# An attention and expert kernel: the key-value step one batch later, one pending projection at the end of the batch, and one scatter then two

## The reference, cut to what matters

```python
x  = L0_attn_x                                   # 16 batches x 256 rows x 128, f32
xn = layernorm(x)
out = x + attention(xn) + experts(xn)

# attention: 16 heads of 8 columns, 64 random features per head
q, k, v = xn@Wq + bq, xn@Wk + bk, xn@Wv + bv     # split into heads
qp = relu(q @ rw) + 1e-6                         # per head 8 -> 64
kp = relu(k @ rw) + 1e-6
kv  = einsum('bhsf,bhsd->bhfd', kp, v)
qkv = einsum('bhsf,bhfd->bhsd', qp, kv)
norm = einsum('bhsf,bhf->bhs', qp, kp.sum(axis=2))
attention = (qkv / (norm[..., None] + 1e-6)).reshape(B, S, D) @ Wo + bo

# experts: 8 experts, hidden size 512, each row goes to its best one
logits = xn @ wr + br
gate = p1 / (p1 + p2)                            # the two largest probabilities
experts = gate * (gelu(xn @ w1[e] + b1[e]) @ w2[e] + b2[e])   # e = argmax(logits)
```

## Time and profile before

| | us |
|---|---|
| median of 3 runs | 218.1 (217.13 to 218.14) |
| the profiled execution | 218.47 |
| its span, first to last instruction | 216.4 |
| PE busy | 201.2 (93%) |
| POOL busy | 140.7 (65%) |
| DVE busy | 131.1 (61%) |
| ACT busy | 124.1 (57%) |
| mean granted clock of PE | 0.982 of full |

### The profile page before, as it was taken

How to read it: one execution, slowest core, us unless ns; L and a number is a source line. 1 busy time by engine, 2 the same in 40 slices (tenths; PEclk the granted TensorE clock), 3 DMA queues, 4 the chain that set the end, 5 groups by cost and what they waited for, 6 DMA issues and landing times. The chain is left out here.

```text
span 216.4 us, 6736 instructions
## 1 busy us (share of the span) xinstructions
PE 201.2 (93%) x2291; PEld 162.8 (75%) x2291; DVE 131.1 (61%) x422; ACT 124.1 (57%) x293; POOL 140.7 (65%) x163
## 2 busy tenths in 40 slices
PE   6789996989999999999999999999999999999960
PEld 6466764556676676767766767999999999999960
DVE  5877744779777666677777673554544445544440
ACT  3366988345546655556556585656665555666520
POOL 2498941232188877878778510078888888888885
PEclk9999999699999999999999999999999999999996
DMA  4929999990012111112114882199999999999141
GB/s 134 272 48 266 213 116 255 299 233 6 3 49 64 64 61 55 46 52 64 64 50 114 270 231 70 48 232 199 178 207 215 204 215 199 194 213 198 10 36 10
DMA packets 32192, 29.53 MB, mean 136 GB/s; under 512 B 5505, under 2 KB 24481, under 8 KB 32161
## 3 DMA queue, kind: packets, MB, share of 16 engines
q1 hardware_dynamic: 25520, 24.88, 46.1%
q0 software_dynamic: 6640, 4.24, 12.3%
HBM read 20.17 MB, written 11.49 MB: 146 GB/s over the span
## 5 line engine op out<-in xcount | busy, mean ns | idle before, releaser
L412 POOL DMA_INDIRECT out<-k_all,slots_all x39 | 61.1, 1567 | 23.6 <-issue 23.3
L738 ACT ACTIVATE q_all<-feat,w_slot 128x128 f32<-128x128 f32 x156 | 44.5, 368 | 28.3 <-PE feat L591 20.8
L591 PE MATMUL feat<-v_all,w_slot 128*128 128x128 f32 x312 | 41.2, 275 | 0.0
L380 POOL DMA_INDIRECT sorted_x<-rows_all,place_i x32 | 31.9, 995 | 13.0 <-PE feat L477 8.0
L591 PEld LDWEIGHTS feat<-v_all,w_slot 128*128 128x128 f32 x312 | 38.0, 192 | 0.0
L695 ACT ACTIVATE k_feat<-feat 128x1024 f32<-128x1024 f32 x16 | 16.4, 1024 | 19.8 <-PE feat L477 19.8
L702 ACT ACTIVATE q_feat<-feat 128x1024 f32<-128x1024 f32 x16 | 16.4, 1027 | 15.5 <-PE feat L488 15.5
L884 DVE TENSOR_SCALAR q_feat<-feat 128x1024 f32<-128x1024 f32 x16 | 19.6, 1225 | 8.8 <-PE feat L488 8.8
L488 PE MATMUL feat<-q_all,rw_bd 32*128 32x256 f32 x256 | 18.8, 408 | 3.8 <-DVE k_feat L877 1.9
L337 POOL TENSOR_SCALAR rows_all<-x_all,meanvar,rstd 128x128 f32<-128x128 f32 x21 | 16.8, 811 | 7.8 <-DVE rstd L770 7.7
L601 PE MATMUL o_bank<-w_sb,q_all 128*128 x160 | 21.2, 275 | 0.0
(11 more groups left out here) (120 smaller groups left out, 314.5 us busy)
## 6 DMA issues: line engine op xcount, KB each, us to landing
w_slot<-w1x SPq DMA_DIRECT2D x39, 258.0 KB
sorted_x<-ones_f SPq DMA_DIRECT2D x1, 2535.0 KB, 20.2
x_all<-in_x SPq DMA_DIRECT2D x8, 256.0 KB, 4.1
w1x<-in_w SPq DMA_DIRECT2D x1, 2048.0 KB, 25.6
out<-res SPq DMA_DIRECT2D x16, 128.0 KB
slots_all<-sorted_x SPq DMA_DIRECT2D x23, 65.0 KB
out<-k_all,slots_all POOLq DMA_INDIRECT x39
slots_all<-sorted_x SPq DMA_DIRECT2D x1, 520.0 KB, 5.1
```

The costliest lines, as they stand in the source:

```text
L380: pool.indirect_dma_start(sorted_x, bass.IndirectOffsetOnAxis(ap=place_i[:, t:t + 1], axis=0), rows_all[:, t, :], None).then_inc(x_moved, 16)
L412: pool.indirect_dma_start(out_rows, bass.IndirectOffsetOnAxis(ap=slot_rows[j % SLOT_RING][:, D + 1:XW].bitcast(I32), axis=0), y_sb[j % Y_R ...
L591: ins = pe.matmul(bank[:, a * P:(a + 1) * P], w1_slot[j % W1_RING][:, a * P:(a + 1) * P], xsT[j % X_RING][:, :], start=True, stop=True)
L738: act.activation(hidden_T[j % H_RING][:, a * P:(a + 1) * P], hid_bank[j % HID][:, a * P:(a + 1) * P], ACT.Gelu, bias=w1_slot[j % W1_RING][ ...
```

## The change

In stage 2 KV of a batch is issued one pass later: `key_values(i-1)` between O and QF; the last one follows the loop. WO moves from before QF to the end of the pass. On DVE `mask_kv(i-1)` stands ahead of `q_relu(i)`, `residual` is taken one pass later (`i-5`), and three pieces of the routing go from before `q_relu` to after `token_rows`. On POOL the scatters of a pass are one at KF and two at QF instead of two and one (the total is 32 as before), `out_bias(i-1)` comes after those two, and the sixteen `add_out_bias` are done in the passes 0 to 3, four each. In stage 1 POOL normalises 2, 1 and 2 tiles of the chunks 1 to 3 instead of 3 each, and ACT saves the first transposed chunk before the second square root.

```diff
-KF_MOVES = {i: 2 for i in range(FIRST_MOVES, 15)}
-QF_MOVES = {i: 1 for i in range(FIRST_MOVES, 14)}
+KF_MOVES = {i: 1 for i in range(FIRST_MOVES, 14)} | {14: 2}
+QF_MOVES = {i: 2 for i in range(FIRST_MOVES, 14)}
...
-NORM = [0] + [3] * (CHUNKS - 1)
+NORM = [0, 2, 1, 2] + [3] * (CHUNKS - 4)
@@ POOL, the loop over the batches
                 pool.wait_ge(kf_ps, i + 1)
                 moves(KF_MOVES.get(i, 0))
-                if i >= 1:
-                    out_bias(i - 1)
                 if i + 1 < NBATCH:
                     spread_v(i + 1)
                 pool.wait_ge(qf_ps, i + 1)
                 moves(QF_MOVES.get(i, 0))
-                add_out_bias(i)
+                if i >= 1:
+                    out_bias(i - 1)
+                if i < FIRST_MOVES:
+                    for b in range(NBATCH // FIRST_MOVES * i, NBATCH // FIRST_MOVES * (i + 1)):
+                        add_out_bias(b)
@@ PE, the loop over the batches
                 if i >= 2:
                     outputs(i - 2)
+                if i >= 1:
+                    key_values(i - 1)
+                q_features(i)
+                if i >= 2:
+                    turn_outputs(i - 2)
+                if i >= 1:
+                    turn(i)
                 if i == 4:
                     pe.wait_ge(placed, 2)
                     pe.wait_ge(wo_in, 16)
                 if i >= 4:
                     out_project(i - 4)
-                q_features(i)
-                if i >= 2:
-                    turn_outputs(i - 2)
-                if i >= 1:
-                    turn(i)
-                key_values(i)
+            key_values(NBATCH - 1)
@@ ACT, stage 1
             deviation(0)
+            save_xnT(0)
             deviation(1)
-            save_xnT(0)
             deviation(2)
@@ DVE, the loop over the batches
-                if i == 1:
-                    count_slots()
-                if i == 2:
-                    place_rows()
-                if i == 3:
-                    place_gates()
-                if i >= 4:
-                    residual(i - 4)
+                if i >= 5:
+                    residual(i - 5)
+                if i >= 1:
+                    mask_kv(i - 1)
                 if i == 4:
                     compare_slots()
...
                 if i >= 2:
                     token_rows(i - 2)
-                mask_kv(i)
                 if i == 1:
+                    count_slots()
                     find_first()
+                if i == 2:
+                    place_rows()
+                if i == 3:
+                    place_gates()
+            mask_kv(NBATCH - 1)
+            residual(NBATCH - 5)
```

## The result

The changed kernel took 220.24 us (median; 219.97 to 220.54) where the kernel before took 218.10: a ratio of 1.0109, with a 95% interval of 1.0077 to 1.0141. The forecast was 216.8, faster. Two later comparisons, on two more chips, gave 1.0095 (1.0064 to 1.0126) and 1.0121 (1.0079 to 1.0164). It is about 1% slower each time.

What follows compares the result with a forecast made beforehand. PE's own work was taken to bound the attention loop, the relu chain close behind. Terms 0.9 + 0.2 - 1.35 - 2.2 + 0.2 + 0.7 + 0.2 = -1.35 gave 217.1 us profiled, 216.8 median; range 215.2 to 219.9.

Steps and rivals of the forecast that it cites:

- The loop, passes 5 to 14: Attention loop: about 5.57 us a pass instead of 5.87; -1.35 for passes 5 to 7, -2.2 for 8 to 14.
- KF(2): Start of the attention: lower clock until about 44.4 us puts KF(2) at 47.3 instead of 46.37, 0.9 later.
- KF(1): Start of the attention: KF(1) no longer waits behind KV(0), its input ready at about 40.4 us against 40.88.
- Passes 2 to 4: Early attention passes: 17.3 us instead of 17.07, +0.2, with place_rows making one pass 0.5 longer.
- The first slot: After the loop: +0.7 behind KF(15) as KV(15) follows the loop, +0.2 for the sorted rows' later load.
- Stage 1: Before the attention: fewer POOL tiles let the third chunk's transposes start sooner; 0.1 us gained, bounds 0.8 less to 0.3 more.
- KF completes late: Rival, attention loop: the pair of scatters holds KF's completion back by 0.65, a pass is 5.8, total 219.8 us; chance 0.26.
- The clock rises in time: Rival, start of attention: lower clock ends at 41.4 as before, KF(2) at 45.9, total 215.4 us; chance 0.16.
- The change does not do what it says: Rival: O and KV do not join (1.4 us back) and sorted rows land late (0.5), total 218.6 us; chance 0.11.

Runs made afterwards that it cites:

- the kernel with three edits: Changed kernel with KV(0) back in pass 0, one output-bias addition per pass and weight loads behind the store of batch 8: 221.05 us, 1.0113 of the kernel before.
- the dummies: Changed kernel with 17 dummy transposes behind KF(0) and 12 behind QF(0) in pass 0: 217.08 us, 0.9964 of the kernel before.

## Why the prediction was wrong, step by step

- **The loop, passes 5 to 14: right.** A pass was forecast at 5.57 and took 5.54. O and KV do join. KF to QF is 2.96 to 2.98, forecast 3.0. The rule of the Trainium skill that only a change of the tiling mode drains the engine (TensorEngine Tiling (Array Packing), Key Properties) agrees with this trace: O is followed by KV after 0.89, the same 16 matmuls that took 1.00 ahead of a group with other tiles. These terms gave 3.75 us where 3.35 was expected.
- **KF(2), +0.9 forecast, +2.26 measured: the mechanism right, one bound wrong.** QF(1) was put at 45.0 and started at 45.11. The next step failed: "I expect the lower clock until about 44.4", and so "KF(2) 2.6 behind it". The half clock lasted until 47.1, QF(1) took 2.09 instead of 1.15, and KF(2) came 3.52 behind it. I had read the length of the stretch from one fall and one rise; in other profiles it is 0, 3.4 or 6.8 us. The term should have had the whole of pass 1 at the lower clock as its bound. With it, KF(2) would have come out at 48.5 and the sum 1.2 higher. (The prediction also calls a rule of the Trainium skill a voice against this part; as it words the rule, the rule supports the cost that it computed.)
- **KF(1) gained nothing by losing KV(0).** The prediction gave the kernel before 40.88 for it, held by KV(0), and 40.4 without. It stood there because KV(0) itself ran at half clock; in the profiles at full clock KF(1) follows it at 40.40 to 40.45 with 0.73 to spare. The step removed a cover for PE and no cost.
- **Passes 2 to 4, +0.2 forecast, +1.32 measured: a cost left out.** "`place_gates` is shorter and costs nothing" and, of POOL, "free": each was costed by itself, and at the durations of the kernel before. `count_slots`, the third piece that moves, has no price in the prediction at all, and its pass has the largest miss: passes 2 to 4 were put at 5.6, 6.1 and 5.6 and took 6.25, 6.08 and 6.06. Only `place_rows`, the piece that was costed, came out as forecast. Before, the additions stood one by one; four in a row now cover just the stretch in which DVE's steps run between the relus. The pair costs 18.39 - 17.25 = 1.14, and vanishes with either part: 17.25 with the additions spread, 17.12 with the steps back at their old place.
- **The first slot, +0.9 forecast, +2.31 measured.** The issue of the rows was forecast at KF(14) + 9.7 = 126.7 and was at 126.19. What failed is "the rows need some 2.3 to land": 2.3 was the landing on idle DMA engines, and the order put it right behind six loads of weights. The slot at KF(15) + 6.52, without that, is the 6.55 of the prediction.
- **Stage 1** gave 0 of the expected 0.1: KF(0) at 34.55, before 34.49.
- **The rivals.** "KF completes late" did not happen in the first measurement, and did on two other chips, at first with the price that it was given: 0.5 to 0.55 late, 5.64 and 5.71 a pass, where the prediction's chain gives 5.66 to 5.71. At 0.65 it gives 5.8, and the kernel with three edits took 5.97, since KV was late as well, which the rival left out. Its total of 219.8 also holds a slip: three passes of 5.8 are 17.4 and not 17.8, so the rival's own time is 219.4. "The clock rises in time" is what the dummies made: KF(2) at 45.73, forecast 45.9. "The change does not do what it says" is out: the order does what it says, and the rows did land late, its second half; the slot lost 1.4 more than forecast where the rival gave 0.5.
- **The sum.** -1.35 forecast; +1.36 for the clock, +1.12 for passes 2 to 4, +1.41 for the slot, -0.4 for the loop and the rest: +2.1. All three misses are of one kind, a duration taken over from another place: the steps and the landing from where their neighbours were idle, the half clock from the one stretch in which it had been seen.

The range ended at 219.9, and 220.24 lies outside. The prediction had one or two bad terms at a time, and none of them was passes 2 to 4; three moderate ones together were not in it.

## What to carry to other kernels

A duration from a trace holds together with what ran beside it: when a step is moved, look up what the other engines, the DMA queues and the clock do at its new place. Moving work out of a place where an engine waits gains nothing there and may lower PE's clock; the work left in the hole is worth keeping. And when a reordering is a large gain in its loop and a loss at both ends, take the ends back one by one: here the new order with KV(0), the routing steps and the start of the weight loads put back was 0.7 and 0.9% faster than the kernel before on two chips without late groups, where the whole change was 1% slower. On a chip with late groups it was level, with dummies that themselves cost some time. A reordering is therefore worth measuring on more than one chip.

## What was not expected of the hardware

- Small DVE operations beside POOL's tensor operations took 0.43 to 0.66 us instead of 0.17, while POOL's 0.70 did not grow (four in 2.78).
- The stretch at half clock behind the same waits of PE lasted 3.4 or 6.8 us in profiles of kernels with the same code up to there, and nothing in between; with KV(0) in pass 0 also 0.
- A group of matmuls that completes while POOL issues scatters can reach the other engines 0.5 to 1.3 us late, and the matmuls behind it are stretched (QF 1.15 to 1.96 or 2.34). It came on some chips for an order that showed none on others: for the changed kernel in two comparisons of three, with the scatter at the same distance from KF (0.16 and 0.20 us behind its start in the two profiles with late groups, 0.16 in the first, without). On one chip the late groups moved from KF to KV and QF when the pair of scatters was moved from QF to KF, the pass grew from 5.64 to 6.37 us, and the passes without scatters had none; so scatters are part of it. What makes a chip or an order prone to it is open.
